# First attention and long convolution in one block of a float32 two-layer kernel: the heads of the convolution inside the attention's steps

## The chip, the cores and the metric

The kernel runs on one core of one Trainium2 chip. The metric is the device time of one execution in microseconds (us). A difference of about 1% is what a measurement of this kernel can tell from none.

## The reference

Two transformer layers on `x` of 16 batches, 128 positions, 256 channels, all float32. The change touches the first two sublayers; the experts, the wide attention, the linear attention and the expert mix stay.

```python
x = x + _L0_attn_ref(_layernorm(x), ...)                 # LoRA attention, 16 heads of 16 channels
x = x + _L0_xattn_ref(ctx_2048, ctx_2048, _layernorm(x), ssm_kernel, D, 8)   # long convolution
x = x + _L0_ffn_ref(_layernorm(x), ...)                  # LoRA experts, and so on
...
# _L0_attn_ref: q, k, v = lora_linear(x); per batch and head
scores = jnp.einsum('bhqd,bhkd->bhqk', q, k) * SCALE
attn = jax.nn.softmax(scores, axis=-1)
out = jnp.einsum('bhqk,bhkd->bhqd', attn, v)             # then lora_linear with Wo
...
# _L0_xattn_ref: k, v are the context, 16 heads of 8 channels, 256 positions
kv = jnp.einsum('bhil,bhjl->bijhl', k_, v_)
y = irfft(rfft(kv, n=2 * L) * rfft(ssm_kernel, n=2 * L), n=2 * L)[..., :L]
out = y + kv * D[None, None, None, :, None]
out = jnp.einsum('bijhl,bhil->bjhl', out, q_)            # q is the normalised x
```

The attention needs the whole row of `x`; the convolution of `kv` needs only the context, and its last product (`out` with `q_`) needs the attention's result for that batch.

## The kernel before

**Names.** `G = 4` batches make a group, `NG = 4` groups make the 16 batches. PE is TensorE, DVE VectorE, ACT ScalarE, POOL GpSimd; each runs its own instructions in the order in which they are written, and waits on semaphores that the others raise. A float32 product "with a high and a low part" is three matmuls (`product`, lines 41 to 43).

**Attention (`stage_lora_attention`).** A prologue loads and splits the weights and projects group 0. Then 64 steps follow, `n = 16 g + u`: group `g`, step `u` of the group. A step treats 4 of the 16 heads of one batch, 16 steps are a group. In the loop over `n` each engine does its part of several neighbouring steps:

- PE: `turn(n)` (4 transposes of the probabilities, line 353), every second step `scores` for two later steps (line 343), `weigh(n - 1)` (probabilities times values, line 365), every fourth step `project` (the output projection), and in `extra` the transposes and the q, k, v projections of the next group.
- ACT: `exps` (line 508), two steps ahead, and the copies out of PSUM.
- DVE: `inverse_sums(n + 1)` (reciprocal, line 576), `row_max(n + 3)` (line 571), `keep_probT(n)` (copy out of PSUM, line 581), and at the end of some steps the norm of a later group: `vector_stats` at `u = 3` (line 111), `vector_apply` at `u = 6` (line 125).
- POOL: `normalise(n + 1)`, the product of 512 probabilities with the inverse sums (line 275), the power for the norm (`pool_rstd`, line 132), the bias (`add_bias`, line 270), and in group 2 the pair products of the first convolution group (line 284).

So one step's chain is reciprocal on DVE, `normalise` on POOL, `turn` on PE, copy on DVE. What DVE does at the end of a step stands ahead of the next step's reciprocal.

**Convolution (`stage_long_conv`).** A block of its own behind a barrier of all engines. For each group: pair products of the context's 8 channels (36 pairs, lines 674 and 810), on PE three matmuls of 144 columns for each of 16 heads with the Toeplitz matrix `toep` (lines 772 to 774), the copies to `y` on ACT (line 819), on DVE 15 products of `y` with the normalised and transposed `x` into 8 slots (lines 870 and 874, together some 10 us), on PE 64 transposes that sum the slots in PSUM (line 784), and four adds to `x` (line 849). Both inputs of the 15 products lie in SBUF. The block ends with the norm for the experts.

The order of everything is written out by hand; loops over groups in the convolution are hardware loops (`Fori`), those of the attention are unrolled.

## Time and profile before

| | |
|---|---|
| median of 3 runs | 1102.06 us (1100.9 to 1110.97) |
| profiled execution, span from the first to the last instruction | 1105.4 us |
| prologue of the attention, to the first copy of turned probabilities | 33.8 us |
| 64 attention steps and what follows, to the convolution's block | 170.1 us |
| convolution, to the first matmul of the experts | 106.0 us |
| experts | 83.0 us |
| the rest | 712.5 us |

The profiled execution has no time of its own beside its span. Its span is 3.3 us (0.3%) above the median of the runs, and inside their range. TensorE's granted clock was 0.935 of full speed over the span; in the profile 1.00 is 2.4 GHz and 0.50 is 1.2 GHz.

### The profile page before, as it was taken

The page shows a single profiled execution, that of the slowest core. Times are in us where ns is not written, and L with a number is a line of the kernel's source. Part 1 is how long each engine was busy: PE and PEld are TensorE (multiplying, and loading weights), DVE is VectorE, ACT ScalarE, POOL GpSimd, SP SyncE. Part 2 cuts the span into 40 slices and gives each one's busy share as a digit, 9 for nine tenths or more (in the row PEclk, how much of TensorE's full clock was granted, in tenths as well). Part 3 has the DMA queues.
Part 4 walks back from the last instruction along what each step waited for, and adds up shares of the span by engine and source line. Part 5 has one row for each costly group of instructions (what it writes and reads, how often), then busy time and mean ns, then how long its engine had stood idle before and what let it go on. Part 6 is the DMA issues. An engine that isn't in the chain of part 4 may idle for free. (4 is left out here: it accounts for less than half of the span.)

```text
span 1105.4 us, 20085 instructions
## 1 busy us (share of the span) xinstructions
PE 986.7 (89%) x7437; PEld 850.5 (77%) x7437; DVE 647.0 (59%) x1392; ACT 479.1 (43%) x1587; POOL 262.6 (24%) x247
## 2 busy tenths in 40 slices
PE   8898999788855389999999999999999977999977
PEld 6666776688755368888888988889888866777757
DVE  5576667378677834544455445645455455677854
ACT  3576775323234124444444444444444444434521
POOL 3353774244055401111111111111111112011000
PEclk9698996989887689999999999999999999989979
DMA  7000000000053010000000000000000006000002
GB/s 280 2 1 2 1 2 1 21 1 1 1 171 115 19 42 1 1 1 1 0 0 0 0 0 0 0 0 0 1 1 1 1 4 241 1 2 2 2 1 76
DMA packets 10518, 27.56 MB, mean 25 GB/s; under 512 B 1936, under 2 KB 7088, under 8 KB 9808
## 3 DMA queue, kind: packets, MB, share of 16 engines
q1 hardware_dynamic: 9728, 26.42, 6.9%
q8 instruction: 45, 0.74, 0.3%
q10 hardware_dynamic: 720, 0.20, 0.1%
q14 instruction: 25, 0.20, 0.1%
HBM read 24.52 MB, written 2.10 MB: 24 GB/s over the span
## 5 line engine op out<-in xcount | busy, mean ns | idle before, releaser
L1158 POOL TENSOR_TENSOR wa_prob<-wa_prob,wa_rsum 128x512 f32<-128x512 f32 x64 | 66.9, 1045 | 443.6 <-DVE wa_rsum L1375 443.6
L41 PE MATMUL bank<-norm_xT_hi,wide_hi 128*128 128x512 f32 x256 | 106.8, 417 | 2.2 <-ACTq L1342 2.2
L1302 ACT ACTIVATE wa_prob<-wa_prob,wa_negmax 128x128 f32<-128x128 f32 x256 | 100.0, 391 | 17.5 <-DVE wa_negmax L1364 17.2
L1401 DVE TENSOR_TENSOR le_w_or_z_lo<-bank,le_w_or_z_hi 128x512 fp32r<-128x512 f32 x64 | 44.2, 691 | 105.6 <-ACT le_w_or_z_hi L1335 104.9
L43 PE MATMUL bank<-norm_xT_hi,wide_lo 128*128 128x512 f32 x256 | 101.8, 398 | 0.0
L42 PE MATMUL bank<-norm_xT_lo,wide_hi 128*128 128x512 f32 x256 | 101.6, 397 | 0.0
L508 ACT ACTIVATE v_or_conv<-bank,la_negmax 128x128 f32<-128x128 f32 x256 | 90.4, 388 | 6.9 <-PE bank L353 5.1
L1317 ACT COPY wa_v<-bank 128x512 f32<-128x512 f32 x64 | 37.4, 585 | 127.8 <-PE bank L43 127.8
L1310 ACT COPY wa_q<-bank 128x512 f32<-128x512 f32 x64 | 37.5, 586 | 115.6 <-PE bank L43 115.6
L275 POOL TENSOR_TENSOR v_or_conv<-v_or_conv,la_rsum 128x512 f32<-128x512 f32 x64 | 66.4, 1040 | 80.4 <-DVE la_rsum L576 80.3
L1370 DVE COPY wa_k<-bank 128x512 f32<-128x512 f32 x64 | 44.2, 691 | 68.3 <-PE bank L43 68.3
L41 PE MATMUL bank<-wide_hi,le_w_or_z_hi 128*128 128x256 f32 x256 | 73.3, 286 | 1.7 <-DVE le_w_or_z_lo L1401 1.4
L1388 DVE COPY wa_probT<-bank 128x512 f32<-128x512 f32 x64 | 44.1, 688 | 51.3 <-PE bank L1220 51.3
L42 PE MATMUL bank<-wide_lo,le_w_or_z_hi 128*128 128x256 f32 x256 | 71.7, 280 | 0.0
L43 PE MATMUL bank<-wide_hi,le_w_or_z_lo 128*128 128x256 f32 x256 | 71.5, 279 | 0.0
L1230 PEld LDWEIGHTS bank<-wa_probT,wa_v 128*128 128x128 f32 x512 | 65.9, 191 | 7.1 <-DVE wa_probT L1388 2.6
L1230 PE MATMUL bank<-wa_probT,wa_v 128*128 128x128 f32 x512 | 67.9, 275 | 0.7 <-DVE wa_probT L1388 0.7
L1182 PE MATMUL bank<-wa_k,wa_q 128*128 128x128 f32 x512 | 67.6, 275 | 0.0
L132 POOL TENSOR_TENSOR norm_rstd<-norm_rstd,minus_half 128x4 f32<-128x4 f32 x23 | 24.0, 1045 | 179.2 <-DVE norm_rstd L118 179.1
L1182 PEld LDWEIGHTS bank<-wa_k,wa_q 128*128 128x128 f32 x512 | 62.7, 192 | 0.5
L581 DVE COPY v_or_conv<-bank 128x512 f32<-128x512 f32 x64 | 43.9, 686 | 30.6 <-PE bank L353 30.5
L508 ACT ACTIVATION_READ_ACCUMULATOR v_or_conv<-bank,la_negmax 128x1 f32 x256 | 58.3, 228 | 0.0
(282 smaller groups left out, 2567.7 us busy)
## 6 DMA issues: line engine op xcount, KB each, us to landing
le_raw<-in_wide_w SPq DMA_DIRECT2D x16, 512.0 KB, 4.1
em_w<-in_em_w SPq DMA_DIRECT2D x1, 4096.0 KB, 15.4
x<-in_x SPq DMA_DIRECT2D x4, 512.0 KB, 4.7
lc_kt<-in_ctx_rev SPq DMA_DIRECT2D x1, 2048.0 KB, 10.1
lc_toep<-in_toeplitz SPq DMA_DIRECT2D x1, 2048.0 KB, 14.5
out_x<-x SPq DMA_DIRECT2D x8, 256.0 KB, 2.9
li_kt<-in_ctx_rev SPq DMA_DIRECT2D x1, 1536.0 KB, 7.6
la_w_raw<-in_l_w SPq DMA_DIRECT2D x1, 1024.0 KB, 6.4
```

What stands on the lines that cost most here:

```text
L41: nc.tensor.matmul(out, a[0], b[0], start=start, stop=False, skip_group_check=True)
L42: nc.tensor.matmul(out, a[0], b[1], start=False, stop=False, skip_group_check=True)
L43: return nc.tensor.matmul(out, a[1], b[0], start=False, stop=stop, skip_group_check=True)
L275: nc.gpsimd.tensor_tensor(own, own, rsum[:, n % NS, :].unsqueeze(2).to_broadcast([P, 4, P]), ALU.mult)\
L508: last = nc.scalar.activation(prob[:, n % NP, s, :], b_s[n % RG][:, s * P:(s + 1) * P], ACT.Exp, bias=negmax[:, n % NS, s:s + 1], accum_ou ...
L1158: nc.gpsimd.tensor_tensor(prob[:, s], prob[:, s], rsum[:, s, :].unsqueeze(2).to_broadcast([P, G, P]), ALU.mult).then_inc(prob_ok, 1)
L1182: last = nc.tensor.matmul(b_s[s][:, t], q[:, s, t], k[:, s, t], start=True, stop=True)
L1230: last = nc.tensor.matmul(b_z[:, j * P:(j + 1) * P], v[:, g % 2, j, m * HD:(m + 1) * HD], probT[:, h % 2, j, :], start=True, stop=True)
L1302: last = nc.scalar.activation(prob[:, s, j, :], prob[:, s, j, :], ACT.Exp, bias=negmax[:, s, j:j + 1], scale=SCALE, accum_out=sums[:, s, j ...
L1370: nc.vector.tensor_copy(k[:, s, :], b_p[1][:, :]).then_inc(k_ok, 1)
L1388: nc.vector.tensor_copy(probT[:, t % 2], b_t[:, :].rearrange("p (j k) -> p j k", j=G))\
L1401: nc.vector.tensor_tensor(z[1][:, t % 2, :], b_z[:, :], z[0][:, t % 2, :].bitcast(F32), ALU.subtract).then_inc(z_lo, 1)
```

## The change

One block takes the place of both. What was the convolution is spread over the attention's steps:

- **PE.** `conv(n - 4)` stands right behind `turn(n)` in every step from 4 to 67: one head of the convolution as a matmul of 288 columns and one of 144, into a single bank, so it waits until ACT has copied the head before. Behind it in PE's order stand `scores`, `weigh`, `project` and `extra`. The scores have 3 banks, not 4, and are asked for one step later. For a group two groups back the slots are summed by `add_up` at `u = 1` and `u = 2` (32 transposes, not 64); the transposes of the convolution's normalised `x` stand at `u = 6` and 7.
- **DVE.** From group 1 on, `fill` writes the slots of the group before, one slot (two products) at the end of each step `u = 9` to 14, two at 15. A second norm (`cnorm`) has its statistics at `u = 4` and its result at `u = 5`, and the norm for the experts moves into groups 2 to 3 (`u = 3`, `u = 8`). `add_skip` moves from group 3 to group 0.
- **POOL.** In each step, behind `normalise`, one or two of the 28 pair products of a group; at `u = 11`, 13, 15 and the next `u = 0` `add_slots`, a sum of two slots of 1024 columns; one more power for a norm in each group.
- **ACT.** In each step the copy of one head (`keep_conv`), every fourth step the squares.
- The loop goes on for 16 steps past the last softmax, and the last group's slots are filled and summed after it. The barrier between the blocks goes. The context and the Toeplitz matrix are loaded in four parts each, among the groups of `x`; the experts' weights are loaded in this block.

```diff
@@ GpSimd, in the loop over n
-            for n in range(N - 1):
+            for n in range(N + U):
                 g, u = divmod(n, U)
-                normalise(n + 1)
+                if n + 1 < N:
+                    normalise(n + 1)
...
+                if n < N:
+                    pair_products(n // 4, QUARTER[n % 4])
+                if g + 1 < NG and 10 <= u < 10 + G:
+                    add_bias(g + 1, u - 10)
+                if 2 <= g <= NG and u == 0:
+                    add_slots(g - 2, 3)
+                if 1 <= g < NG and u in (11, 13, 15):
+                    add_slots(g - 1, (u - 11) // 2)
...
+            def add_slots(i, p):
+                pool.wait_ge(slot_ok, C * i + 2 * p + 2)
+                nc.gpsimd.tensor_tensor(slot[:, p], slot[:, p], slot[:, 4], ALU.add).then_inc(add_ok, 1)
@@ TensorE
+            def conv(c):
...
+                wait(pe, c_ok, c)
+                cols = G * NPAIR
+                both = kk[:, m % 2, :, G * hl:G * hl + G, :].rearrange("p a b n -> p a (b n)")
+                nc.tensor.matmul(b_c[:, 0:2 * cols], toep[:, h, 0:P], both, start=True, stop=False,
+                                 skip_group_check=True)
+                nc.tensor.matmul(b_c[:, cols:2 * cols], toep[:, h, P:2 * P], both[:, 0], start=False, stop=True,
+                                 skip_group_check=True).then_inc(c_ps, 1)
...
-            for n in range(N + ADD_AT):
+            for n in range(N + U):
                 g, u = divmod(n, U)
                 if n < N:
                     turn(n)
-                    if n % 2 == 0 and n + RG < N:
-                        scores(n + RG)
+                c = conv_due(n, CONV_AT)
+                if c is not None:
+                    conv(c)
+                if n % 2 == 1 and n + 3 < N:
+                    scores(n + 3)
                 if 1 <= n <= N:
                     weigh(n - 1)
@@ VectorE
+            def fill_slot(i, s, buffer):
...
+                ins = nc.vector.tensor_tensor(own[:, :, s:C], yv[:, :, OFF[s]:OFF[s] + C - s], qv[:, :, 0:C - s],
+                                              ALU.mult)
...
+            def fill(i, s):
+
+                if s % 2 == 1:
+                    wait(dve, add_ok, 4 * i + s // 2)
+                fill_slot(i, s, 4 if s % 2 else s // 2)
...
+                if g >= 1:
+                    if u == 4:
+                        dve.wait_ge(x_ok, G * g)
+                        cnorm.vector_stats(dve, g - 1)
+                    if u == 5:
+                        cnorm.vector_apply(dve, g - 1)
+                if 1 <= g < NG:
+                    for s in SLOT_AT.get(u, ()):
+                        fill(g - 1, s)
```

with `SLOT_AT = {9: (0,), 10: (1,), 11: (2,), 12: (3,), 13: (4,), 14: (5,), 15: (6, 7)}`.

What stands on the engines in steps 27 and 28 (group 1, `u = 11` and 12) shows the three moves.

DVE before, steps 27 and 28, each from its reciprocal on:

```order
L576 RECIPROCAL la_rsum<-la_sums 128x4
L571 TENSOR_REDUCE la_negmax<-bank 128x4
L148 TENSOR_TENSOR la_xT_lo<-bank,la_xT_hi 128x512
L581 COPY v_or_conv<-bank 128x512
L576 RECIPROCAL la_rsum<-la_sums 128x4
L571 TENSOR_REDUCE la_negmax<-bank 128x4
L581 COPY v_or_conv<-bank 128x512
L592 TENSOR_TENSOR x<-bank,x 128x256
```

DVE of the change, the same two steps:

```order
L735 RECIPROCAL la_rsum<-la_sums 128x4
L149 TENSOR_TENSOR la_xT_lo<-bank,la_xT_hi 128x512
L740 COPY la_probT<-bank 128x512
L729 TENSOR_REDUCE la_negmax<-bank 128x4
L769 TENSOR_TENSOR la_slots_or_raw<-la_y,la_cxT 128x128x6
L773 TENSOR_TENSOR la_slots_or_raw<-la_y,la_cxT 128x128x2
L735 RECIPROCAL la_rsum<-la_sums 128x4
L729 TENSOR_REDUCE la_negmax<-bank 128x4
L740 COPY la_probT<-bank 128x512
L751 TENSOR_TENSOR x<-bank,x 128x256
L769 TENSOR_TENSOR la_slots_or_raw<-la_y,la_cxT 128x128x5
L773 TENSOR_TENSOR la_slots_or_raw<-la_y,la_cxT 128x128x3
```

The two products of a slot, both with two inputs in SBUF, stand at the end of each step, ahead of the next reciprocal; in the odd step the row maximum comes behind the copy.

POOL before, steps 27 and 28 and the first instruction of the next:

```order
L275 TENSOR_TENSOR v_or_conv<-v_or_conv,la_rsum 128x512
L270 TENSOR_TENSOR x<-x,la_out_bias 128x256
L275 TENSOR_TENSOR v_or_conv<-v_or_conv,la_rsum 128x512
L270 TENSOR_TENSOR x<-x,la_out_bias 128x256
L275 TENSOR_TENSOR v_or_conv<-v_or_conv,la_rsum 128x512
```

POOL of the change, the same two steps and the first instruction of the next:

```order
L317 TENSOR_TENSOR la_prob<-la_prob,la_rsum 128x512
L328 TENSOR_TENSOR h_or_w<-la_kt 128x32
L312 TENSOR_TENSOR x<-x,la_out_bias 128x256
L335 TENSOR_TENSOR la_slots_or_raw<-la_slots_or_raw 128x1024
L317 TENSOR_TENSOR la_prob<-la_prob,la_rsum 128x512
L328 TENSOR_TENSOR h_or_w<-la_kt 128x32x7
L328 TENSOR_TENSOR h_or_w<-la_kt 128x32x6
L312 TENSOR_TENSOR x<-x,la_out_bias 128x256
L317 TENSOR_TENSOR la_prob<-la_prob,la_rsum 128x512
```

Between one `normalise` (line 317) and the next there are now two or three more instructions, one of 1024 columns in step 27.

PE before, step 28 and the start of 29:

```order
L353 MATMUL bank<-ident,v_or_conv 128x128 x4
L343 MATMUL bank<-la_k,la_q 128x128 x8
L365 MATMUL bank<-v_or_conv 32x128 x4
L353 MATMUL bank<-ident,v_or_conv 128x128 x4
L365 MATMUL bank<-v_or_conv 32x128 x4
```

PE of the change, steps 28 and 29 (lines 41 to 43 here are the k projection of the next group):

```order
L410 MATMUL bank<-ident,la_prob 128x128 x4
L455 MATMUL bank<-h_or_w,la_toep 128x288
L457 MATMUL bank<-h_or_w,la_toep 128x144
L422 MATMUL bank<-la_probT,la_v 32x128 x4
L41 MATMUL bank<-norm_xT_hi,w_or_z_hi 128x512
L42 MATMUL bank<-norm_xT_lo,w_or_z_hi 128x512
L43 MATMUL bank<-norm_xT_hi,w_or_z_lo 128x512
L410 MATMUL bank<-ident,la_prob 128x128 x4
L455 MATMUL bank<-h_or_w,la_toep 128x288
L457 MATMUL bank<-h_or_w,la_toep 128x144
L400 MATMUL bank<-la_k,la_q 128x128 x8
L422 MATMUL bank<-la_probT,la_v 32x128 x4
```

The head of the convolution (lines 455 and 457) stands between the transposes and what follows them in every step.

## Rows read from the trace of the kernel before

**Rows 1.** Windows: length, busy us of each engine, clock, DMA share, GB/s.

```profile
0.00:33.81 33.81, 26.20 (x122) 20.23 (x124) 18.14 (x49) 14.69 (x42) 10.19 (x14) 0.96 0.63 230
33.81:78.63 44.82, 41.24 (x386) 31.07 (x384) 28.36 (x70) 28.68 (x137) 20.94 (x22) 0.84 0.01 2
78.63:122.91 44.28, 39.64 (x402) 30.19 (x403) 29.26 (x73) 30.47 (x145) 20.45 (x22) 0.92 0.01 2
122.91:162.41 39.50, 36.46 (x398) 27.65 (x398) 25.80 (x57) 29.90 (x144) 30.03 (x36) 1.00 0.01 1
162.41:203.89 41.48, 34.74 (x322) 24.67 (x322) 30.73 (x83) 22.20 (x118) 15.57 (x15) 0.75 0.01 2
203.89:309.94 106.05, 88.52 (x680) 86.74 (x680) 67.31 (x139) 29.53 (x63) 30.37 (x22) 0.90 0.02 6
```

**Rows 2.** Timeline, TensorE, attention steps 31 to 34: start, us, engine, line.

```profile
122.27 0.60 PE L353 MATMUL bank<-ident,v_or_conv 128*128 128x128 f32 x4
122.80 1.16 PE L343 MATMUL bank<-la_k,la_q 32*128 32x128 f32 x16
123.89 0.42 PE L365 MATMUL bank<-v_or_conv 128*32 128x128 f32 x8
124.24 0.66 PE L137 MATMUL bank<-ident,norm_xn 128*128 128x128 f32 x4
...
127.08 0.50 PE L41 MATMUL bank<-la_xT_hi,la_w_hi 128*128 128x512 f32 x1
...
128.57 0.60 PE L353 MATMUL bank<-ident,v_or_conv 128*128 128x128 f32 x4
```

**Rows 3.** Timeline, TensorE, end of a convolution group.

```profile
238.47 0.41 PE L774 MATMUL bank<-v_or_conv,lc_toep 128*128 128x144 f32 x2
238.71 7.15 PE L784 MATMUL bank<-ident,lc_yq 128*128 128x128 f32 x64
```

**Rows 4.** Timeline, VectorE, products of a convolution group.

```profile
227.98 2.22 DVE L870 TENSOR_TENSOR lc_yq<-v_or_conv,lc_xT 128x1024 f32<-128x1024 f32 x2
...
230.42 1.07 DVE L870 TENSOR_TENSOR lc_yq<-v_or_conv,lc_xT 128x768 f32<-128x768 f32 x1
...
237.10 1.09 DVE L874 TENSOR_TENSOR lc_yq<-v_or_conv,lc_xT 128x896 f32<-128x896 f32 x1
```

**Rows 5.** Timeline, VectorE and GpSimd, both in SBUF-to-SBUF products.

```profile
218.74 1.09 DVE L674 TENSOR_TENSOR v_or_conv<-lc_kt 128x896 f32<-128x896 f32 x1 [14.85 <-PE bank L774]
218.78 2.17 POOL L674 TENSOR_TENSOR v_or_conv<-lc_kt 128x512 f32<-128x512 f32 x1 [6.45 <-PE bank L774]
219.75 2.14 DVE L674 TENSOR_TENSOR v_or_conv<-lc_kt 128x768 f32<-128x768 f32 x1
220.92 1.94 POOL L674 TENSOR_TENSOR v_or_conv<-lc_kt 128x384 f32<-128x384 f32 x1
```

**Rows 6.** Groups on GpSimd: count, busy us, mean ns of one, idle before.

```profile
L275 POOL TENSOR_TENSOR v_or_conv<-v_or_conv,la_rsum 128x512 f32<-128x512 f32 x20 | 20.8, 1039 | 14.7 <-DVE la_rsum L576 14.6
L284 POOL TENSOR_TENSOR v_or_conv<-lc_kt 128x256 f32<-128x256 f32 x2 | 1.5, 730 | 0.0
L284 POOL TENSOR_TENSOR v_or_conv<-lc_kt 128x128 f32<-128x128 f32 x2 | 1.0, 516 | 0.0
...
L940 POOL TENSOR_TENSOR wide_lo<-le_raw,wide_hi 128x1024 fp32r<-128x1024 f32 x16 | 37.7, 2382 | 9.2 <-ACT wide_hi L990 9.2
```

**Rows 7.** Timeline, a norm in step 19, and the wait behind it.

```profile
88.66 1.40 DVE L111 BATCH_NORM_STATS2 norm_stats<-x 128x6 f32<-128x256 f32 x4
...
92.84 1.12 PE L353 MATMUL bank<-ident,v_or_conv 128*128 128x128 f32 x4 [1.88 <-POOL v_or_conv L275]
```

**Rows 8.** Windows, the same stretch.

```profile
91.00:94.00 3.00, 1.16 (x8) 0.83 (x12) 2.26 (x7) 1.84 (x9) 2.78 (x3) 0.73 0.00 0
94.00:97.00 3.00, 3.00 (x14) 2.15 (x15) 1.35 (x3) 0.00 (x0) 1.04 (x1) 0.50 0.00 0
```

**Rows 9.** Timeline, VectorE, last x update of the group before the last.

```profile
290.21 1.42 DVE L849 TENSOR_TENSOR x<-bank,x 128x256 f32<-128x256 f32 x4 [8.20 <-PE bank L784]
```

746 lines of the change are left out of this document (363 added, 383 removed).

## The prediction

> **What bounds the kernel now.** I read the windows by stage first, then the timeline of each engine in the stretch that the change touches, then the groups on GpSimd. In the windows [rows 1] group 2 of the attention (122.9 to 162.4) is the clean one: full clock, no norm of a later group on VectorE, and TensorE busy for 36.5 of 39.5 us, while VectorE has 25.8, ScalarE 29.9 and GpSimd 30.0. The convolution keeps TensorE busy for 88.5 of its 106.1 us. So TensorE bounds both blocks, and putting them together saves no column of work; what it can win is TensorE's idle time (17.5 us in the convolution, 18.0 in the four groups of steps) and the serial stretches at a block's ends. Everything up to the first matmul of the experts lies on the path that sets the end; nothing behind that point changes. The sum is therefore made for that stretch, 309.9 us in the profiled execution, and the difference is added to the median of 1102.1. The profiled span is 0.3% above the median, which is less than the terms below are uncertain by.
>
> **TensorE's work.** A step of the attention is 0.53 us of transposes, half of 1.09 us of scores and 0.35 us of weighing, together 1.43, and six matmuls of a projection take 1.49 us [rows 2]. A convolution matmul of 144 columns takes 0.24 us [rows 3], a head has three, 0.73 us. The change's 288 and 144 columns are the same 432 columns, so also 0.73. The slot sums fall from 64 transposes a group to 32 for three of the groups; at 7.15 us for 64 [rows 3] that is 3.5 us each.
>
> **Prologue: 33.8 us, as before** [rows 1]. The same weights and projections, in a slightly different order. The loads that are new ahead of step 0 (a second group of x, a quarter of the context, a quarter of the Toeplitz matrix, 1.5 MB) are 6.5 us at the 230 GB/s that the prologue shows, and that queue has some 20 us for them. Nothing is put down for the later loads: the DMA share is 0.01 and 0.02 in the rest.
>
> **Group 0: 52 us.** Before 44.8. It gains 12 heads, 8.8 us. TensorE idles for 3.6 us of this group, and I let that swallow half its size: 7 us. Adding the skip term (16 small VectorE instructions) comes from group 3; VectorE is busy here for 28.4 of 44.8 us, so it is hidden; if it isn't, it costs what it saves in group 3.
>
> **Light steps of groups 1 to 3 (u = 0 to 8).** A clean step is 39.5 / 16 = 2.47 us, with a head 3.20, nine steps 28.8. Then the norms. A norm puts statistics of 1.40 us and more on VectorE at a step's end [rows 7], ahead of the next reciprocal; the power on GpSimd stands ahead of the next normalise; and TensorE stood for 1.88 us in front of the next transposes. Group 1 has one such norm and took 44.3 us, group 2 none and took 39.5: 4.8 us for a norm, the drop of the clock behind it included. The change has two norms in groups 1 and 2 (u = 3 and 8, u = 4 and 5) and one in group 3. Heads on TensorE fill part of the wait: 8 us for two, 4 for one. Group 1: 28.8 + 8 = 36.8.
>
> **Heavy steps of groups 1 to 3 (u = 9 to 15).** Here the change puts VectorE's 15 products with two inputs in SBUF, 10.2 us (227.98 to 237.10 and 1.09) [rows 4], beside GpSimd instructions that read SBUF as well. The trace has that pairing: VectorE's 768 columns take 1.07 us alone [rows 4] and 2.14 beside GpSimd [rows 5]; GpSimd's 512 columns take 1.04 alone [rows 6] and 2.17 beside VectorE [rows 5]. The four instructions of that group run from 218.74 to 222.86, 4.12 us. Their lengths alone are 1.09 (896 columns), 1.04 (512), 1.07 (768) and by the line below some 0.9 (384), together 4.1: they ran one after the other, each waiting for the whole of the other engine's.
>
> So in these seven steps the two engines' instructions are added. GpSimd [rows 6]: 7 normalise at 1.04 are 7.3; 12 pair products of 224 to 32 columns, by the line through 0.73 us at 256 and 0.52 at 128, 6.0; 4 biases of 256 columns at 0.73, 2.9; 3 slot sums of 1024 columns at 2.38 (the only row of that size, though with another output type), 7.1. That is 23.3, and with 10.2 of VectorE 33.5 us. TensorE needs less: 7 x (1.43 + 0.73) = 15.1, a k half 1.5, the values 3.0, two output projections 1.5, transposes 0.5, in all 21.6. It can't run ahead, since each step's transposes want that step's normalise, and normalise stands in GpSimd's row behind the slot sum of the step before. VectorE's product of the sixth slot waits for the slot sum of the step before, and the eighth for one in its own step; behind them stands the next reciprocal. I take 33.5, 4.8 us a step. The bounds are 22.4 (seven steps of 3.20, nothing of this on the path) and 39 (half of VectorE's other work in seven steps, 25.8 / 16 x 7 = 11.3 us, beside nothing of GpSimd's).
>
> The Trainium skill, page "SBUF — State Buffer", section "Who interferes with whom", says that a VectorE instruction with two SBUF inputs contends with a GpSimd instruction that reads SBUF, and that who comes second is blocked for the whole instruction. By that rule the heavy steps are a sum over both engines; without it they would be TensorE's 22. The rows of the collision agree with it.
>
> **The groups.** Group 1: 36.8 + 33.5 = 70.3. Group 2 adds 3.5 of slot sums on TensorE and, at u = 0, a slot sum on GpSimd, of which 1.5 stick out: 75.3. Group 3 has no next group: three projections of 1.5 fewer in the light steps, one norm fewer (4), no biases (2.9): 63.9.
>
> **Tail: 27 us.** Past step 63 come four heads, the last output projection and its update, some 5 us. From then on the chain is the one the convolution ends with today: add to x, statistics, power, result, 15 products, sums, adds, next block, from 290.21 [rows 9] to 309.94 [rows 1], 19.7 us. The change has the two transposes and copies of x inside it, 2.2 us. The splitting of the experts' weights also moves here, beside the products; 1040 columns on GpSimd are 2.4 us by the row of 1024, hidden if the order is kind: 0 to 2.4, I take 0.
>
> **New waits.** A head waits for ScalarE's copy of the head before, and behind it on TensorE stand scores, weighing and projections. All copies of the convolution are inside ScalarE's 29.5 us of that block, 7.4 a group; with 29.9 of a clean group it has 37.3 us of work in 64 to 75. I take 0; at worst all of the 29.5 us comes out on TensorE's path. It can't be a gain, since no wait goes for it. Three score banks let the row maximum start only 0.53 + 0.73 + 1.09 = 2.35 us behind an odd step's transposes; with the maximum and the rest of the chain that is under two steps' 6.4, so 0, and worse only at half clock.
>
> **Sum.** 33.8 + 52 + 70.3 + 75.3 + 63.9 + 27 = 322.3 us, against 309.9: 12.4 longer. The forecast is 1102.1 + 12.4, about **1114 us**.
>
> **Rivals.**
> *TensorE stays the bound.* The instructions interleave so that the shared reads don't reach the path, and a heavy step costs 3.20. Then 3 x 11.1 = 33 us go: 289 us, 1081. For it: GpSimd was idle 14.7 us in front of normalise in group 2 and the steps around it [rows 6], and it waits for nobody but the reciprocal. Against it: GpSimd's own 23.3 is already more than 22.4, before any product.
> *Half of it.* Collisions take half of their price, 16 us less: 1098.
> *The clock.* In a heavy step of over 6 us (u = 13, 15) TensorE has 3 us of work. Where it was busy for 1.16 of 3 us, the granted clock was 0.73 and then 0.50, that is 1.2 GHz [rows 8]. If that happens in each heavy stretch and lasts, TensorE's 21.6 us become 43, and from the point where they pass 33.5 TensorE decides: some 10 us in each of three groups, 1145, clearly slower. Against it: the convolution's matmuls give TensorE work in every step; group 3, which has half clock for much of its length today (0.75) [rows 1], may be better off.
> *The convolution isn't hidden at all.* Every head and every product come on top of the steps: 33.8 + 170.1 + 106.1 less the barrier between the blocks (some 2 us), 308: 1100. The block would do nothing that it says. For it: both blocks are bound by the same engine. Against it: TensorE's idle 18 us among the steps can take heads. Its chance is counted with "half of it".
>
> **How the numbers follow.** Forecast (1104 to 1125) 0.42; half of it (1090 to 1103) 0.20; TensorE the bound (1068 to 1089) 0.17; the clock (1126 to 1150) 0.17; elsewhere 0.04. The range reaches from inside the third to inside the fourth: 1076 to 1140. About 1% is what a measurement of this kernel tells from no change, so faster is under 1091: the third case and a part of the second, 0.24. Slower is over 1113: the clock, and a little over half of the forecast's case, 0.43. Between them 0.33.
>
> **What would show it.** Right: heavy steps of 4.5 us and more, products of VectorE and GpSimd's instructions longer than the rows above, TensorE idle in front of its transposes with GpSimd as releaser, groups of some 70 us in 1 and 2, the experts' first matmul at 315 to 330 us. The norm step is right if u = 3 to 6 show TensorE waiting for over 1 us twice. Wrong: heavy steps near 3.2 us, or products at their old durations. What would upset the forecast most is a GpSimd that runs its pair products in the shadow of VectorE's PSUM reads, so that hardly any collide.

## The result

The changed kernel takes 1121.6 us (median; 1117.7 to 1123.8) against 1101.5 in the same comparison: ratio 1.019, with an interval of 1.016 to 1.023. So it is slower by 20 us. The forecast was 1114 in a range of 1076 to 1140. Where a ratio to the kernel before is given, its 95% interval follows it; a time from one run has none.

The profiled execution has a span of 1121.7 us, before 1105.4. These are the windows by stage of the changed kernel, cut where [rows 1] is cut: prologue, groups 0 to 3, the tail behind the last softmax, the experts, the rest. Columns: start and end, length, busy us (and instructions) of PE, of PE's weight loads, of DVE, ACT and POOL, then clock, DMA share, GB/s.

```profile
0.00:34.61 34.61, 20.41 (x120) 16.12 (x120) 16.96 (x48) 14.65 (x42) 10.11 (x14) 1.00 0.68 244
34.61:89.33 54.72, 48.81 (x436) 37.02 (x434) 34.56 (x88) 33.95 (x153) 32.32 (x51) 0.94 0.01 1
89.33:156.85 67.52, 55.20 (x484) 41.81 (x484) 48.33 (x101) 40.70 (x179) 42.87 (x53) 0.97 0.00 1
156.85:225.04 68.19, 55.59 (x504) 43.11 (x504) 49.86 (x104) 38.13 (x166) 46.02 (x55) 1.00 0.01 1
225.04:281.00 55.96, 45.01 (x412) 34.55 (x412) 41.56 (x81) 27.43 (x128) 39.83 (x48) 0.91 0.01 2
281.00:317.72 36.72, 21.46 (x122) 18.49 (x123) 20.68 (x38) 4.00 (x9) 6.77 (x4) 0.75 0.00 0
317.72:401.00 83.28, 45.29 (x192) 41.63 (x192) 62.98 (x143) 26.27 (x45) 42.02 (x20) 0.68 0.31 101
401.00:1121.70 720.70, 683.87 (x4945) 595.69 (x4945) 384.95 (x781) 297.04 (x898) 93.02 (x98) 0.97 0.04 15
```

The experts' first matmul starts at 317.72, before at 309.94: 7.8 us of the 16.3 between the two profiles arise in the changed block. The other 8.5 arise behind it, in code that is the same. (The medians differ by 20.1 us: the kernel before was profiled in an execution 3.3 us above its median.) In groups 1 and 2 no engine is busy for more than 82% of the time: TensorE waits 12 us in each. For what, five rows of the waits of the changed kernel between 30 and 276 us say (who waits <- for whom: us in total, times, the longest):

```profile
POOL la_prob L317 <- DVE la_rsum L735: 87.1, 44, 8.7
DVE la_negmax L729 <- PE bank L400: 31.7, 25, 3.0
PEld bank L410 <- POOL la_prob L317: 22.2, 14, 2.8
PE bank L455 <- ACT la_y L658: 20.8, 31, 1.5
PE bank L410 <- DVE la_probT L740: 12.9, 9, 2.6
```

The fourth row is the wait that the prediction put at nothing: 31 heads wait 20.8 us in all for ScalarE's copy of the head before. The first two rows are idle time of GpSimd and VectorE, which matters only where these set the pace. One of the 31, in the timeline of group 1, `u = 6`:

```profile
112.72 0.60 PE L410 MATMUL bank<-ident,la_prob 128*128 128x128 f32 x4
...
112.92 1.45 ACT L611 ACTIVATE la_q<-bank,la_q_bias,la_parity 128x512 f32<-128x512 f32 x2 [2.71 <-PE bank L43]
...
114.25 0.40 ACT L658 COPY la_y<-bank 128x288 f32<-128x288 f32 x1
...
114.70 0.75 PE L455 MATMUL bank<-h_or_w,la_toep 128*128 128x288 f32 x2 [1.39 <-ACT la_y L658]
```

ScalarE makes its copies of q first (1.45 us), then the copy of the head; only then may the next head start, and TensorE stands for 1.39 us with weighing and the next group's projections behind it (in odd steps the scores too).

### The profile page after: what moved, and what is told of

Same layout as the page of the kernel before. It is cut to its first block and busy times, and to the rows that moved or that the text cites. A ratio compares the mean times of both kernels' runs of the same rounds, so it can differ in the third digit from the quotient of the medians.

```text
span 1121.7 us, 19630 instructions
## 1 busy us (share of the span) xinstructions
PE 975.6 (87%) x7213; PEld 828.4 (74%) x7213; DVE 659.9 (59%) x1379; ACT 482.2 (43%) x1616; POOL 313.0 (28%) x339
## 5 line engine op out<-in xcount | busy, mean ns | idle before, releaser
L1396 DVE TENSOR_TENSOR w_or_z_lo<-bank,w_or_z_hi 128x512 fp32r<-128x512 f32 x64 | 44.3, 692 | 107.1 <-ACT w_or_z_hi L1330 106.4
L635 ACT ACTIVATE la_prob<-bank,la_negmax 128x128 f32<-128x128 f32 x256 | 91.6, 387 | 20.4 <-DVE la_negmax L729 20.4
L317 POOL TENSOR_TENSOR la_prob<-la_prob,la_rsum 128x512 f32<-128x512 f32 x64 | 66.5, 1038 | 87.2 <-DVE la_rsum L735 87.1
L41 PE MATMUL bank<-wide_hi,w_or_z_hi 128*128 128x256 f32 x256 | 73.8, 288 | 1.7 <-DVE w_or_z_lo L1396 1.4
L42 PE MATMUL bank<-wide_lo,w_or_z_hi 128*128 128x256 f32 x256 | 72.2, 282 | 0.0
L43 PE MATMUL bank<-wide_hi,w_or_z_lo 128*128 128x256 f32 x256 | 72.0, 281 | 0.0
L455 PE MATMUL bank<-h_or_w,la_toep 128*128 128x288 f32 x128 | 46.2, 443 | 21.6 <-ACT la_y L658 21.6
L729 DVE TENSOR_REDUCE la_negmax<-bank 128x4 f32<-128x512 f32 x64 | 43.1, 674 | 32.8 <-PE bank L400 32.4
L133 POOL TENSOR_TENSOR norm_rstd<-norm_rstd,minus_half 128x4 f32<-128x4 f32 x19 | 19.9, 1049 | 143.8 <-DVE norm_rstd L119 143.8
```

The costliest lines, as they stand in the source:

```text
L41: nc.tensor.matmul(out, a[0], b[0], start=start, stop=False, skip_group_check=True)
L42: nc.tensor.matmul(out, a[0], b[1], start=False, stop=False, skip_group_check=True)
L43: return nc.tensor.matmul(out, a[1], b[0], start=False, stop=stop, skip_group_check=True)
L317: nc.gpsimd.tensor_tensor(own, own, rsum[:, n % NS, :].unsqueeze(2).to_broadcast([P, 4, P]), ALU.mult)\
L455: nc.tensor.matmul(b_c[:, 0:2 * cols], toep[:, h, 0:P], both, start=True, stop=False, skip_group_check=True)
L635: last = nc.scalar.activation(prob[:, n % NP, s, :], b_s[n % NS_BANKS][:, s * P:(s + 1) * P], ACT.Exp, bias=negmax[:, n % NS, s:s + 1], ac ...
```

## The experiments

Lengths are read from the start of one copy of turned probabilities on VectorE to another's. "Light" are the nine steps `u = 0` to 8, "heavy" the seven from 9 on (in group 3 six, to step 63); "tail" is from step 63 to the experts' first matmul, "rest" from there to the end.

Each column is one profiled execution; the last row is the median of all runs of that kernel.

| us | changed | head at end | head after scores | copy first | eight slots | everything | everything, head in front |
|---|---|---|---|---|---|---|---|
| group 0, light | 29.3 | 24.7 | 29.4 | 29.0 | 27.7 | 24.7 | 29.4 |
| group 0, heavy | 25.4 | 22.5 | 24.6 | 21.6 | 22.5 | 22.5 | 25.4 |
| group 1, light | 35.4 | 27.6 | 31.0 | 29.4 | 27.6 | 27.6 | 36.9 |
| group 1, heavy | 32.2 | 30.7 | 31.0 | 31.6 | 24.2 | 24.2 | 28.0 |
| group 2, light | 36.0 | 33.8 | 36.4 | 32.4 | 34.2 | 34.2 | 39.3 |
| group 2, heavy | 32.2 | 30.7 | 31.0 | 32.0 | 24.1 | 24.1 | 27.9 |
| group 3, light | 29.2 | 31.4 | 35.2 | 33.0 | 31.7 | 31.7 | 32.4 |
| group 3, heavy | 22.5 | 20.6 | 20.6 | 22.0 | 16.6 | 17.0 | 18.3 |
| tail | 41.0 | 40.8 | 41.0 | 39.6 | 38.2 | 31.6 | 30.1 |
| rest | 804.0 | 802.5 | 802.6 | 802.8 | 801.8 | 800.1 | 799.5 |
| median of runs | 1121.6 | 1102.9 | 1117.9 | 1105.9 | 1084.4 | 1074.0 | 1101.8 |

### The head at the end of the step

```diff
-                c = conv_due(n, CONV_AT)
-                if c is not None:
-                    conv(c)
...
                 extra(g, u)
+                c = conv_due(n, CONV_AT)
+                if c is not None:
+                    conv(c)
```

> One edit: the convolution's head stands at the end of TensorE's step, behind the next group's work, and no longer right behind the transposes. In the changed kernel TensorE waits 21.6 us in 32 places ahead of a head for ScalarE's copy of the head before (single bank), a wait that the prediction put at nothing. Theory A (that wait is on the path in the light steps, where TensorE bounds): the copy gets a step's length more, the wait falls under 6 us, the light steps (u = 0 to 8) of groups 1 and 2 fall from 35.4 and 36.0 us to under 33, the heavy ones stay at 32; the whole at 1108 to 1114. Rival B (the head in front fills time in which the turned probabilities are copied; at the end it delays the next transposes by its 0.73 us): light steps 37 us and more, the whole 1126 or more. Rival C (the chain goes over GpSimd and VectorE everywhere): the whole within 4 us of the changed kernel's 1121.6.

Measured: 1102.9 us, ratio to the kernel before 1.002 (0.999 to 1.005). The waits and group 1 go as A has them, and the whole falls further than its 1108 to 1114; group 2's light steps don't, they take 33.8 us (at a clock of 0.90), where A had under 33. The place of the head alone is 19 us, nearly the whole of the change's loss; half clock in other steps of the two profiles accounts for some 2 of that. The waits of heads for the copy, in the same view as above, are a single one:

```profile
PE bank L455 <- ACT la_y L658: 0.4, 1, 0.4
```

The light steps of group 1 fall from 35.4 to 27.6 us. Their windows, changed kernel first, and between them all that TensorE waited for in the changed one:

```profile
89.33:124.68 35.35, 29.40 (x247) 22.11 (x247) 20.31 (x61) 22.65 (x97) 16.85 (x27) 0.95 0.01 1
PE bank L455 <- ACT la_y L658: 6.0, 8, 1.5
81.29:108.91 27.62, 27.30 (x262) 21.55 (x261) 20.67 (x61) 22.43 (x97) 16.77 (x27) 1.00 0.01 2
```

All 6.0 us of TensorE's idle time stood in front of heads; with the head at the end TensorE is busy for 27.3 of 27.6 us. It is the bound of these steps now, and the two norms on VectorE in them cost nothing that shows. The rest of the fall, 1.5 us, is half clock in step 19 of the changed kernel.

### Is it the scores behind the head, or the head's own wait?

```diff
                     turn(n)
+                if n % 2 == 1 and n + 3 < N:
+                    scores(n + 3)
                 c = conv_due(n, CONV_AT)
                 if c is not None:
                     conv(c)
-                if n % 2 == 1 and n + 3 < N:
-                    scores(n + 3)
                 if 1 <= n <= N:
                     weigh(n - 1)
```

> One edit: the head stands behind the scores and ahead of the weighing, where the changed kernel has it ahead of the scores; in even steps, which have no scores, it stands where it stood. At the end of the step it gave 1102.9, against 1121.6 ahead of the scores. Theory A (what costs is that the scores of three steps later stand behind the head and behind its wait for ScalarE's copy: copy, head, scores, row maximum, exponentials is a ring that goes round once in two steps): the first nine steps of group 0 fall from 29.3 us to 25 to 26, the whole to 1101 to 1106, though a head goes on waiting for the copy. Rival B (what costs is the wait for the copy, wherever the head is early in a step): weighing and the next group's projections still stand behind it, the nine steps stay at 28 or more, the whole at 1115 or more.

Measured: 1117.9 us, ratio 1.014 (1.010 to 1.018). By the whole it is B. TensorE was at half clock for two stretches that the kernel with the head at the end doesn't have (steps 1 and 2, 3.0 us; step 55, 7.29 against 3.95 us), 6.3 us that belong to neither theory. The steps say B too. The first nine steps of group 0, which A had at 25 to 26, stay at 29.4 us; without the half clock they take 26.3, which is what they take with the head ahead of the scores at full clock.

In group 1's light steps, at full clock, TensorE is busy for 27.9 of 33.8 us with the head in front (in the kernel with tiny slot sums below, whose group 1 is untouched), for 28.0 of 31.0 behind the scores, and for 27.3 of 27.6 at the end. The idle time is 6.0, 3.1 and 0.3 us, and in the first two all of it stands in front of heads. So what the place costs is the head's own wait: behind the scores it is half as long. That late scores cost anything beside it is not shown.

### ScalarE's copy of the head first in its step

```diff
@@ ScalarE, in the loop over n
+                c = conv_due(n, CONV_AT + 1)
+                if c is not None:
+                    keep_conv(c)
                 b = batch_due(n, HI_AT)
                 if b is not None:
                     keep_o(b)
                 extra(g, u)
-                c = conv_due(n, CONV_AT + 1)
-                if c is not None:
-                    keep_conv(c)
```

> The changed kernel with one edit on ScalarE: the copy of the head stands first in its step, ahead of the copies of q, k, v and of the attention's result, which it stood behind. The head stays right behind TensorE's transposes. Theory A (TensorE's head waits since ScalarE's copy stands behind those other copies): of the 20.8 us in 31 waits of a head for the copy more than half go, step 6 of group 0 (3.39 us) and of group 1 (3.59) falls to under 2.5, the nine steps of group 1 to 31 to 32.5, the whole to 1110 to 1116. Rival B (the copy waits for the exponentials ahead of it, not for those copies): the waits stay over 15 us, the whole within 4 us of 1121.6.

Measured: 1105.9 us, ratio 1.001 (0.999 to 1.004), below A's range. The head stays in front, and yet 16 of the 19 us are gone. The waits between 30 and 262 us:

```profile
PE bank L455 <- ACT la_y L658: 4.0, 6, 1.2
PEld bank L455 <- ACT la_y L658: 3.1, 4, 0.8
```

20.8 us in 31 waits have become 4.0 in 6; the second row, the weight loads ahead of the heads, was 14.6 in 17. Step `u = 6` of group 1, the one shown above, falls from 3.59 to 1.48 us (in the kernel with tiny slot sums, where step 19 has full clock, it takes 2.96). So what cost was mostly that the head waited for the copies of q, k, v and of the attention's result that stood ahead of its own copy.

### Heads of 4 and 2 columns

```diff
+                if i > 0:
+                    cols, both = 2, both[:, :, 0:2]
                 nc.tensor.matmul(b_c[:, 0:2 * cols], toep[:, h, 0:P], both, start=True, stop=False,
```

> Leaves work out: from the convolution's group 1 on, the head's matmuls take 4 and 2 columns in place of 288 and 144; their place and all waits stay, and the heads of group 0 are whole. Theory A (the place in the ring costs: what stands behind the head waits for ScalarE's copy, however short the head is): the nine light steps of group 2 fall from 36.0 us by 2 us or less, and the waits of heads for the copy grow by what the matmuls lose. Rival B (the head's own 0.73 us is on the path): they fall by 5 to 6.6 us (nine heads). In the heavy steps both expect little, under 2 us: VectorE and GpSimd set those.

Measured: 1128.2 us in one run, more than with whole heads. The edit takes less away than its columns say: from its start to the start of what follows, a whole head took 0.8 to 0.9 us, one of 4 and 2 columns 0.4 to 0.5. Steps 20 to 24, the light steps with short heads in group 1, are at full clock, first with whole heads (in the kernel with tiny slot sums), then with short ones:

```profile
104.82:122.85 18.03, 14.57 (x126) 10.80 (x125) 12.51 (x37) 11.05 (x46) 10.87 (x17) 1.00 0.01 2
101.23:117.88 16.65, 12.89 (x125) 9.84 (x123) 12.42 (x38) 11.07 (x45) 10.87 (x17) 1.00 0.01 2
```

TensorE's work falls by 1.7 us, the steps by 1.4; its idle time, all of it in front of heads, is 3.5 and 3.6. So the waits don't grow by what the matmuls lose, as A has it, and most of what the heads lost came off the path, as B has it. The head's wait and its length both stand on the path of the light steps.

In heavy and later light steps the clock differs: TensorE was busy for 1.54 of the 2.80 us of step 24, and steps 25 to 27 ran at 0.64, 0.50 and 0.52, where the changed kernel (1.93 of 2.80 us in step 24) has 1.00. The light steps of group 2 took 39.6, not 36.0 us. On the groups as a whole this run can't decide.

### VectorE's products and GpSimd

Two edits, both for the convolution's groups 1 and 2. One leaves work out: it does 2 of 128 rows (`own[:, 0:rows, s:C]`, and both inputs alike). The other sums as many columns of one input:

```diff
+                if i in (1, 2):
+                    ins = nc.vector.tensor_reduce(own[:, :, s:s + 1], yv[:, :, OFF[s]:OFF[s] + C - s], AX, ALU.add)
+                    if s > 0:
+                        ins = nc.vector.tensor_reduce(own[:, :, 0:1], yv[:, :, OFF[d]:OFF[d] + s], AX, ALU.add)
...
```

> Leaves work out: for the convolution's groups 1 and 2 (attention groups 2 and 3) VectorE's 15 products are done for 2 of their 128 rows only; attention group 1 keeps them whole, as a control. In the changed kernel the heavy steps (u = 9 to 15) take 32.2 us in group 1, 32.2 in group 2 and some 27 in group 3. Theory A (VectorE's products and GpSimd's instructions are added, as the prediction's sum has them): without the 10.2 us of products the heavy steps of group 2 fall to 22 to 25 us, those of group 3 to 18 to 21; group 1 stays at 32. Rival B (something else, TensorE's own work and its waits, bounds the heavy steps): they fall by less than 3 us each. GpSimd's sum of two slots (3.19 us beside a product) falls to 2.4 in both cases.

> Changes work: for the convolution's groups 1 and 2 VectorE's products become sums over the same number of y columns (one input in SBUF in place of two; the result is not the convolution's), attention group 1 keeps the products. Theory A (what costs is that two instructions that both want the shared SBUF read run one after the other): instructions of the same length with one input run beside GpSimd's, and the heavy steps of group 2 fall from 32.2 to 23 to 27 us, nearly as far as with the products left out. Rival B (what costs is VectorE's own time ahead of the next reciprocal): VectorE's time is the same 10 us, so the heavy steps stay at 30 or more while the kernel without the products falls. GpSimd's slot sums: 2.4 us in A.

Measured: the heavy steps of group 2 fall from 32.2 to 26.4 us, by 5.7, with the short products (A had 22 to 25) and to 27.9 with one input (A had 23 to 27, B 30 or more). Those of group 3 (six steps) fall from 22.5 to 17.1 and 18.8, but from a clock of 0.82 to 0.96 and 1.00. Group 1 stays at 32.2 in both. The wholes are 1110.0 and 1110.9, one run each.

In group 2 the 15 products took 17.6 us in the changed kernel, where the kernel before has them at 10.2; the reductions of the same columns take 11.3. So 4.3 us go as soon as one input is dropped, with VectorE as long at it as the products are alone. That the costly thing is the shared read, and not VectorE's own time, is shown as far as reductions, which also write fewer columns, can stand for products. That the two engines' times are added in full is not. These are groups by form from 192 to 225 us, first of the changed kernel, then of the one with one input (count, busy us, mean ns):

```profile
L335 POOL TENSOR_TENSOR la_slots_or_raw<-la_slots_or_raw 128x1024 f32<-128x1024 f32 x3 | 7.9, 2641 | 0.0
L312 POOL TENSOR_TENSOR x<-x,la_out_bias 128x256 f32<-128x256 f32 x4 | 4.1, 1022 | 0.0
L773 DVE TENSOR_TENSOR la_slots_or_raw<-la_y,la_cxT 128x256 f32<-128x256 f32 x1 | 2.6, 2578 | 0.0
```

```profile
L335 POOL TENSOR_TENSOR la_slots_or_raw<-la_slots_or_raw 128x1024 f32<-128x1024 f32 x4 | 9.5, 2378 | 0.0
L312 POOL TENSOR_TENSOR x<-x,la_out_bias 128x256 f32<-128x256 f32 x4 | 2.9, 734 | 0.0
L773 DVE TENSOR_REDUCE la_slots_or_raw<-la_y 128x128 f32<-128x256 f32 x1 | 0.4, 410 | 0.0
```

The 256-column product takes 2.58 us beside a slot sum, as the pairs of [rows 5] did beside each other; the reduction of as many columns takes 0.41; GpSimd's bias falls from 1.02 to 0.73. The Trainium skill, page "SBUF — State Buffer", section "Who interferes with whom", says that a reduction never contends with GpSimd and a two-input VectorE instruction does; the two fences agree.

A short product waits like a whole one: beside a slot sum, one of 8 columns ended when the sum did. With waits like this one the short products still take 4.65 us in group 2, so the edit that shortens them doesn't take all of their cost away.

```profile
208.22 2.38 POOL L335 TENSOR_TENSOR la_slots_or_raw<-la_slots_or_raw 128x1024 f32<-128x1024 f32 x1
...
209.60 1.02 DVE L770 TENSOR_TENSOR la_slots_or_raw<-la_y,la_cxT 128x8 f32<-128x8 f32 x1
```

### GpSimd's slot sums

```diff
+                rows = 2 if i in (1, 2) else 2 * GH
-                nc.gpsimd.tensor_tensor(slot[:, p], slot[:, p], slot[:, 4], ALU.add).then_inc(add_ok, 1)
+                nc.gpsimd.tensor_tensor(slot[:, p, 0:rows], slot[:, p, 0:rows], slot[:, 4, 0:rows], ALU.add)\
+                    .then_inc(add_ok, 1)
```

> Leaves work out: for the convolution's groups 1 and 2 GpSimd's sum of two slots covers 2 of 128 rows; attention group 1 keeps it whole. Theory A (GpSimd's queue sets the heavy steps, and normalise stands behind the slot sum): 7.1 us of GpSimd go from the heavy steps, which fall from 32.2 to 24 to 26 us in group 2 and from 27 to some 20 in group 3. Rival B (the slot sums hide beside TensorE's projections in u = 11, 13, 15): less than 3 us a group. If A holds here and in the kernel without products, both engines' times add up.

Measured: 1109.0 us in one run. Group 2's heavy steps fall to 27.9, 4.3 us, where A has 6 to 8 and B under 3; group 3's fall by 4.0 to 18.5, at a clock of 1.00 and not 0.82. The light steps ahead of them took 39.9 us in group 2, not 36.0, at a clock of 0.87, so the whole says little.

The 4.3 us are not the price of the slot sums. These are the heavy steps of group 2, in the changed kernel, with one input, and with the small slot sums, and then with everything that the next sections change:

```profile
192.88:225.04 32.16, 25.72 (x238) 19.63 (x238) 28.02 (x42) 18.05 (x83) 26.01 (x27) 1.00 0.01 1
193.13:221.02 27.89, 25.07 (x230) 19.55 (x230) 21.80 (x42) 16.75 (x78) 21.54 (x27) 1.00 0.01 1
194.92:222.83 27.91, 25.09 (x230) 19.54 (x230) 23.09 (x42) 16.77 (x78) 19.22 (x27) 1.00 0.01 1
166.41:190.53 24.12, 22.91 (x226) 18.50 (x223) 22.20 (x42) 16.64 (x75) 13.07 (x20) 1.00 0.00 1
```

Two different loads are taken away and both kernels stop at 27.9 us, where TensorE is busy for 25.1 and waits for the other 2.8 in front of heads, for ScalarE's copy. With the short products it is 26.4, of which TensorE is busy for 24.1, and the rest is again in front of heads. So each edit shows how far the next bound lies below 32.2, and not more.

### Eight slots, and another order in the tail

```diff
-                if s % 2 == 1:
-                    wait(dve, add_ok, 4 * i + s // 2)
-                fill_slot(i, s, 4 if s % 2 else s // 2)
+                fill_slot(i, s, s)
...
-                for p in range(4):
+                for p in range(C):
```

with seven slots in one tile and the eighth in `kt[:, 0]`, no `add_slots`, and the head at the end of the step.

> Head at the end of the step, and a buffer for each of the eight slots (the eighth in the first group's context, which is dead by then): GpSimd sums no slots, TensorE turns 64 and not 32 blocks a group. Theory A (VectorE's and GpSimd's instructions are added in the heavy steps): the heavy steps of groups 1 and 2 fall from 30.7 us to 24 to 26, the light ones of groups 2 and 3 gain 3.5 us of transposes, the whole at 1092 to 1097. Rival B (with the head at the end TensorE, at a granted clock of 0.89 there, is the bound of the heavy steps already): they fall by under 3 us, the transposes are added in full, the whole within 3 us of 1103 or above it.

Measured: 1084.4 us, ratio 0.985 (0.981 to 0.989), better than A. The heavy steps of group 1 are 24.2 us, of which TensorE is busy for 23.0; with five slots they were 30.7. Where no head waits, then, the slot sums (7.1 us, and VectorE's waits for them) are worth 6.5. The 32 more transposes don't show in the light steps of group 2 (33.8 and 34.2), since step `u = 1` no longer runs at 0.59 clock.

```diff
@@ TensorE
-                b = batch_due(n, PROJECT_AT)
+                b = NB - 1 if n == N + 1 else batch_due(n, PROJECT_AT) if n < N else None
@@ VectorE, ahead of the adds of step N + 2
+                if n == N + 2:
+                    update(NB - 1)
+                    dve.wait_ge(x_ok, NB)
+                    cnorm.vector_stats(dve, NG - 1)
+                if n == N + 3:
+                    cnorm.vector_apply(dve, NG - 1)
```

and ScalarE's two copies of the experts' weights at step N + 3, again with the head at the end of the step.

> Head at the end of the step, and past the last softmax another order: the last output projection stands ahead of the sums of the group before (64 transposes) on TensorE, its update and the statistics ahead of their adds on VectorE, and the split of the experts' weights follows the projection, not the norm. From step 63's copy to the experts' first matmul the kernel with the head at the end takes 40.8 us. Theory A (the last norm waits for nothing but that projection, and the sums fit into the norm's waits): 32 to 35 us, the whole at 1094 to 1098. Rival B (the tail is bound by TensorE at half clock and by the slots, so what is taken from the front comes back as a wait for the sums): less than 3 us, 1100 to 1103.

Measured: 1092.9 us, ratio 0.994 (0.991 to 0.996); the tail is 32.5 and not 40.8 us: A. In the changed kernel the norm waits behind two blocks of sums (at a clock of 0.74 and 0.82), two heads and the projection:

```profile
282.26 2.34 POOL L335 TENSOR_TENSOR la_slots_or_raw<-la_slots_or_raw 128x1024 f32<-128x1024 f32 x1 [2.65 <-DVE la_slots_or_raw L773]
...
284.65 2.56 PE L478 MATMUL bank<-ident,la_slots_or_raw 128*128 128x128 f32 x16 [2.02 <-POOL la_slots_or_raw L335]
...
288.45 2.32 PE L478 MATMUL bank<-ident,la_slots_or_raw 128*128 128x128 f32 x16
...
292.70 0.42 DVE L751 TENSOR_TENSOR x<-bank,x 128x256 f32<-128x256 f32 x1 [1.20 <-PE bank L43]
293.16 1.40 DVE L112 BATCH_NORM_STATS2 conv_norm_stats<-x 128x6 f32<-128x256 f32 x4
...
301.42 3.88 DVE L769 TENSOR_TENSOR la_slots_or_raw<-la_y,la_cxT 128x1024 f32<-128x1024 f32 x2 [3.73 <-issue]
...
302.46 1.89 POOL L362 TENSOR_TENSOR w_or_z_lo<-le_w,w_or_z_hi 128x784 fp32r<-128x784 f32 x1 [6.18 <-ACT w_or_z_hi L723]
```

With the other order:

```profile
261.98 2.36 POOL L335 TENSOR_TENSOR la_slots_or_raw<-la_slots_or_raw 128x1024 f32<-128x1024 f32 x1 [2.63 <-DVE la_slots_or_raw L774]
...
263.70 0.42 DVE L752 TENSOR_TENSOR x<-bank,x 128x256 f32<-128x256 f32 x1 [1.14 <-PE bank L43]
264.16 1.41 DVE L112 BATCH_NORM_STATS2 conv_norm_stats<-x 128x6 f32<-128x256 f32 x4
264.40 3.29 PE L478 MATMUL bank<-ident,la_slots_or_raw 128*128 128x128 f32 x16 [0.80 <-POOL la_slots_or_raw L335]
...
274.92 2.23 DVE L770 TENSOR_TENSOR la_slots_or_raw<-la_y,la_cxT 128x1024 f32<-128x1024 f32 x2 [4.03 <-ACT la_cxT L145]
```

From the slot sum to the statistics it is 2.2 in place of 10.9 us, and the two first products take 2.23 in place of 3.88: the split of the weights no longer runs beside them.

### Everything, and everything with the head in front

Both together, and GpSimd's biases at `u = 0` to 3 of their own group (`add_bias(g, u)`):

> Head at the end of the step, the other order in the tail, eight slots, and GpSimd's biases in the first four steps of the next group, not in its heavy ones. If the gains add up as the theories of the three kernels have them: 7 us from the tail, 8 from the slots, 2 to 3 from the biases, so 1083 to 1088, and clearly under the kernel before. Rival: TensorE's own work is the floor of the groups (51 us of matmuls in a group of 16 steps, 55 with the projections and transposes of the next group): then the slots and biases give nothing, 1094 to 1097.

Measured: 1074.0 us, ratio 0.978 (0.975 to 0.980), better than forecast. The gains of tail and slots add up (10.0 and 18.5 us apart, 28.9 together); the biases give nothing, the heavy steps are at 24.2 with and without. This version beats the kernel before by 25.5 us and the changed one by 48.

> The kernel with everything (other order in the tail, eight slots, biases in light steps; 1074.0) but with the head where the change has it, right behind the transposes. Theory A (the head's place costs by itself, in light and in relieved heavy steps): 1088 to 1096; the nine light steps of group 1 at 34 to 35.5 us against 27.6, and the seven heavy ones at 26 to 28 against 24.2. Rival B (the place only hurt beside GpSimd's and VectorE's load, which is gone here): 1074 to 1080.

Measured: 1101.8 us, ratio 0.999 (0.996 to 1.002), beyond A's range: the head's place costs 28 us here, 9.3 in the light steps of group 1 (some 3 of it half clock, in steps 19 and 20) and 3.8 in the heavy ones. Of these 28.0 us TensorE is busy for 25.2 and waits 2.8 in front of heads. Where VectorE and GpSimd no longer set the heavy steps, the head's wait does.

### Where TensorE's later instructions lie

```diff
+            for _ in range(64):
+                nc.tensor.matmul(b_v[:, 0:8], lora_b[0:R, 0:P], lora_a[0:R, 0:8], start=True, stop=True)
             pe.wait_ge(loaded, 16 * NLOAD)
```

> The changed kernel with 64 more matmuls of 8 columns in the prologue, into a bank that isn't in use, in a stretch of 6 us in which TensorE waits for the first norm: they do no work that is needed and move all of TensorE's later instructions by 128 places. From the experts' first matmul to the end the kernels with the changed block take 802 to 805 us, the kernel before 795.5, in code that is the same; two steps of that are 1.22 and 1.35 us in which TensorE stands ahead of the scores in the wide attention's loop with nothing to wait for, while a packet of the queue for instructions moves. Theory A (where a loop lies in TensorE's instructions decides whether its jump back finds them loaded): both waits go or change by over 0.5 us, and the number of instruction packets from 400 to 900 us changes from 30. Rival B (a cause in the data or in the clock): the same two waits, the same 30 packets. In the first case the whole moves by 2 to 4 us either way, so the stretch tells, not the whole.

Measured: 1139.6 us, ratio 1.032 (1.026 to 1.037), but for an unmeant reason: the added matmuls took 27.3 us (128 records, 0.21 apart), not 6, and the prologue grew by 19. Behind it the two waits stayed (1.18 and 1.09 us), and so did the packets. As the test was made, A is not confirmed. The last section comes back to it.

## Why the prediction was right, and where it wasn't

**The number.** The forecast had the stretch up to the experts 12.4 us longer; it is 7.8 longer, with 8.5 us behind it that the prediction had excluded. The total was right through terms that erred in both directions; that it came so near is luck. (The chance of 0.24 for faster was also more than its parts give.)

**Prologue** 33.8: 34.6. **Group 0** 52: 54.7, of which 3.0 are steps 1 and 2 at half clock; in the kernel with short heads, whose group 0 is the same code, it is 51.7. The number came out, its reason didn't. Before, steps 0, 1, 4 and 5 of this group ran at 0.50 to 0.62 of full clock, and that is gone at 51.7. In the seven heavy steps all three kernels have full clock. The windows are those of the kernel before and of the one with the head at the end:

```profile
61.72:78.63 16.91, 16.22 (x180) 12.97 (x180) 11.26 (x25) 11.77 (x59) 10.32 (x12) 1.00 0.01 2
58.84:81.29 22.45, 21.88 (x214) 17.88 (x218) 14.65 (x34) 15.41 (x70) 15.95 (x25) 1.00 0.01 2
```

Seven heads are 5.1 us, and the steps grow by 5.5, in the changed kernel by 8.5. Nothing of the heads went into idle time there; that they "swallow half" was luck.

**Light steps** 36.8 in group 1: 35.4. Right size, wrong reason, and this is the step that failed: the norms, "8 us for two", and the new waits, "I take 0". With the head at the end the same norms stand in the same steps and these take 27.6 us, TensorE's busy time. The 8 us are 6.0 of the head's wait for the copy of the head before, and 1.5 of half clock in step 19. The prediction had named the wait and compared ScalarE's sum of work, 37.3 us, with the group's length. That sum says nothing of a wait: the copy is short (0.40 us), but stands behind others. Its sign for the norms did come, TensorE waiting for over 1 us twice in `u = 3` to 6 (1.48 and 1.39), but both are waits for that copy.

**Heavy steps** 33.5: 32.2. The mechanism was there: products took 17.6 us where they had taken 10.2, and one input less brought 4.3. The sum was not. It stood 11.1 us above TensorE's floor of 22.4; in the changed kernel the floor is 27.9, of which 2.8 are the head's wait and 25.1 TensorE's own work, put at 21.6. So the two engines made 4.3 us of a heavy stretch (5.7 by the short products), not 11.1, and where the head stands last the slot sums alone 6.5. The sum came out near since TensorE's work and waits filled what was left over.

**Group 2** 75.3: 68.2. The prediction took its light steps at 41.8; they are 36.0, 2.2 above those of group 1 at full clock, where "slot sums on TensorE 3.5" and "1.5 at u = 0" had 5.0. With the head at the end, where no wait takes them up, 64 transposes of 7.15 us add 6.6 (34.2 against 27.6). **Group 3** 63.9: 56.0.

**Tail** 27: 36.7. The term was "four heads, the last output projection and its update, some 5 us"; from 281.0 to 292.7 that is 11.7, because the sums of the group before stand ahead of the projection. And the split of the experts' weights, put at 0 "if the order is kind", lay beside the first products: 1.65 us.

**Rivals.** "TensorE stays the bound" is wrong for the changed kernel and is what one gets once the head's place, the slot sums and the tail are put right: 1074. "Half of it" was nearer on the collisions than the forecast (4.3 to 5.7 of 11.1 us), but had no wait of the heads to make up for it. "The clock" at length did not come, as the full clock of group 2 shows; the short stretches of it cost 3 us at a time. "Not hidden at all" had 308 us up to the experts; the changed kernel takes 317.7, so in time it hides nothing, and only kernels with the wait or the load taken away are below that (305.4 with the copy first, 296.9 with the head at the end, 270.8 with everything).

**Behind the experts' first matmul.** "Nothing behind that point changes" was right for the code and wrong for the time: 804.0 against 795.5 us. Part of it is named below, 2.6 us. The clock is lower too, 0.68 in the experts, where it was 0.73 before. The cause of that, and of the 4 us or more that every kernel with the changed block has too much (799.5 at the least), stays open. Each of these times is from one profiled execution, and the medians of the kernel before alone go from 1099.5 to 1103.3 us between comparisons, so 4 us may be no effect of the change at all.

## What to carry to other kernels

When a step gets a new instruction that waits for a buffer, look at what stands ahead of the release on the releasing engine, not at that engine's sum, and at everything that is queued behind the waiter. Put such an instruction last in the step, or its release first: each alone gave back 16 to 19 us here. And when a load is taken away to price it, look at what the stretch is then bound by: three kernels stopped at 27.9 or 28.0 us because TensorE and the head's wait were next, and the slot sums were worth 4.3 us there and 6.5 where the head stood last.

## What the runs showed of the hardware

**The same loop, fetched or not.** The wide attention's loop on TensorE is a hardware loop of three rounds. In it TensorE stands twice ahead of the scores with nothing to wait for, one round (128 us) apart. The timeline of the changed kernel has one of the two (the other is 1.35 us at 674.24):

```profile
545.93 1.15 PE L1177 MATMUL bank<-wa_k,wa_q 128*128 128x128 f32 x8 [1.22 <-issue]
```

In the microsecond ahead of it one packet of the queue for instructions moves. From 400 to 890 us that queue has, in the kernel before, the changed one and the one with everything:

```profile
q8 instruction: 13, 0.21, 0.2%
```

```profile
q8 instruction: 29, 0.48, 0.4%
```

```profile
q8 instruction: 12, 0.20, 0.2%
```

The kernels with 12 or 13 packets have neither of the waits (before, eight slots, everything with either place of the head), the others with 29 to 31 have both. All three with eight slots have 96 more transposes on TensorE ahead of the loop. So code ahead of a loop seems to change what its rounds cost, though the padding of 128 records did not. The Trainium skill, page "Runtime: NRT & Kernel Launch", section "Instruction fetch mechanics", says that instructions come in blocks of 16 KiB, 256 instructions each, and that a jump to a block that isn't held waits for it. The packets here agree in size, 0.48 MB in 29. By that page 128 matmuls with as many weight loads are one whole block, so that padding would leave the loop where it lay within its block (an estimate from the page's figure). That fits all the runs, but no run here pads by another length, so the cause is argued and not shown.

**Less work for TensorE, a slower kernel.** With heads of 4 and 2 columns the kernel took 1128.2 us (one run, granted clock 0.901), with whole heads 1121.6 (0.938 in the profiled run). What half clock is worth, [rows 8] had hinted at. The windows of steps 1 and 2 show it, in the changed kernel and then with the head at the end:

```profile
36.49:39.14 2.65, 2.65 (x28) 1.71 (x30) 2.29 (x6) 1.33 (x8) 2.13 (x4) 0.54 0.01 3
39.14:43.44 4.30, 4.30 (x20) 2.90 (x20) 1.12 (x3) 1.44 (x6) 2.52 (x5) 0.50 0.01 2
```

```profile
36.03:38.37 2.34, 2.34 (x34) 1.60 (x33) 2.32 (x7) 1.33 (x8) 2.02 (x4) 1.00 0.02 7
38.37:40.06 1.69, 1.69 (x12) 1.26 (x11) 1.24 (x5) 1.02 (x5) 1.69 (x4) 1.00 0.00 0
```

Heads begin at step 4, so these steps are the same code in both; 1.2 GHz here and 2.4 there is 2.9 us that no edit explains.
